# Decoder kernel, first stage: projection and finished chunk's norm moved to the chunk borders

## What is computed

```python
h_norm = _rmsnorm(h, norm1_w)
out = gate * _causal_conv(h_norm, k_base_kernel)
qk = h_norm @ jnp.concatenate((u, v), axis=1)
q, k = _l2norm(q_raw), _l2norm(k_raw)
A = jnp.einsum('bir,bjr,rij->bij', q * alpha, k, w)        # w: decays, causal mask
out = (out + jnp.einsum('bij,bjd->bid', A, h_norm)) @ proj_w.T + proj_b
h2 = residual + out
hn2 = _rmsnorm(h2, norm2_w)
mlp_out = jax.nn.gelu(hn2 @ mlp_w1 + mlp_b1) @ mlp_w2 + mlp_b2
...
x = _layernorm(x + h2 + mlp_out)                            # then cross-attention, experts
```

## Time and profile before

| | us |
|---|---|
| three runs, median (lowest to highest) | 1377.22 (1376.03 to 1378.42) |
| the profiled execution, its own time | 1376.68 |
| its span, first to last instruction | 1374.5 |
| head, to the first score matmul | 298.9 |
| PE busy in the span | 1194.8 (87%) |
| DVE, ACT, POOL busy | 886.2, 725.4, 239.2 |
| mean granted clock of PE | 0.92 |

### The profile page before, as it was taken

One profiled execution on the slowest core, in us unless ns is written; L12 is line 12 of the kernel. 1 busy time (PEld: TensorE's weight loads), 2 busy tenths in 40 slices (PEclk: granted clock), 3 DMA queues, 4 the chain that ended last, 5 costly groups with the idle time before them and its releaser, 6 DMA issues. The chain is left out here.

```text
span 1374.5 us, 19434 instructions
## 1 busy us (share of the span) xinstructions
PE 1194.8 (87%) x6246; PEld 997.2 (73%) x6246; DVE 886.2 (64%) x1988; ACT 725.4 (53%) x1279; POOL 239.2 (17%) x293
## 2 busy tenths in 40 slices
PE   4687969759999999999999999999646999999960
PEld 2465656747877778787788788788536999999960
DVE  4535343578776567877566877755665777777747
ACT  3424343637667333767433566733324777777744
POOL 1110101000000000000000000000014656666623
PEclk9788888979999999999999999999757999999985
DMA  7201000000000000000000000060560111111144
GB/s 262 70 0 46 1 24 0 24 24 1 1 0 1 32 16 8 1 0 1 32 8 11 6 0 1 1 245 31 183 215 24 47 46 42 42 42 42 46 135 133
DMA packets 45481, 63.46 MB, mean 46 GB/s; under 512 B 7201, under 2 KB 35555, under 8 KB 45283
## 3 DMA queue, kind: packets, MB, share of 16 engines
q1 hardware_dynamic: 40244, 50.52, 11.2%
q0 software_dynamic: 4416, 12.06, 2.9%
q10 hardware_dynamic: 754, 0.03, 0.0%
HBM read 50.21 MB, written 12.39 MB: 46 GB/s over the span
## 5 line engine op out<-in xcount | busy, mean ns | idle before, releaser
L77 PE MATMUL x_psum<-x_s_lo,x_kq_hi 128*128 128x512 f32 (+1 forms) x312 | 126.0, 404 | 8.0 <-PEq L241 4.3
L77 PE MATMUL x_psum<-x_p_lo,x_v_hi 128*128 128x512 f32 (+1 forms) x312 | 124.4, 399 | 0.0
L78 PE MATMUL x_psum<-x_s_hi,x_kq_lo 128*128 128x512 f32 (+1 forms) x312 | 123.4, 396 | 0.0
L79 PE MATMUL x_psum<-x_p_hi,x_v_hi 128*128 128x512 f32 (+1 forms) x312 | 123.3, 395 | 0.0
L78 PE MATMUL x_psum<-x_p_hi,x_v_lo 128*128 128x512 f32 (+1 forms) x312 | 123.3, 395 | 0.0
L79 PE MATMUL x_psum<-x_s_hi,x_kq_hi 128*128 128x512 f32 (+1 forms) x312 | 123.2, 395 | 0.0
L1186 DVE CUSTOM_DVE_ANT_0 x_e<-x_psum,x_rsb,x_rs 128x512 f32<-128x512 f32 (+1 forms) x117 | 86.4, 747 | 48.9 <-PE x_psum L79 47.9
L1036 POOL TENSOR_TENSOR x_sq<-x_sq 128x512 f32<-128x512 f32 x12 | 15.5, 1291 | 578.4 <-ACT x_sq L1022 578.4
L77 PE MATMUL e_bank<-e_w_lo,e_g_hi 128*128 128x256 f32 x368 | 107.7, 293 | 0.1
L77 PE MATMUL e_bank<-e_xT_lo,e_w_hi 128*128 128x256 f32 x368 | 105.0, 285 | 2.3 <-DVE e_xT_lo L1915 1.4
L78 PE MATMUL e_bank<-e_xT_hi,e_w_lo 128*128 128x256 f32 x368 | 104.7, 284 | 0.0
(11 more groups left out here) (353 smaller groups left out, 3284.1 us busy)
## 6 DMA issues: line engine op xcount, KB each, us to landing
w<-in_w SPq DMA_DIRECT2D x16, 1024.0 KB, 12.5
w<-scratch_results SPq DMA_DIRECT2D x8, 512.0 KB, 7.8
x_rsb<-scratch_thin_inv SPq DMA_DIRECT2D x12, 256.0 KB, 3.9
x_rsb<-scratch_thin_rs SPq DMA_DIRECT2D x9, 256.0 KB, 3.9
h_x<-in_x SPq DMA_DIRECT2D x4, 512.0 KB, 6.0
sT<-in_xT SPq DMA_DIRECT2D x4, 512.0 KB, 7.2
h_w<-in_mlp_w SPq DMA_DIRECT2D x2, 1024.0 KB, 10.3
scratch_x<-h_x SPq DMA_DIRECT2D x4, 512.0 KB, 3.3
```

What stands on the lines that cost most here:

```text
L77: pe.matmul(out, w_hi, x_lo, start=start, stop=False)
L78: pe.matmul(out, w_lo, x_hi, start=False, stop=False)
L79: return pe.matmul(out, w_hi, x_hi, start=False, stop=stop)
```

## The change

On every engine the order of the head is rewritten; the arithmetic is the same.

- `project(c + 1)` and `take_projected(c + 1)` go from f = 1 of body c to the border before it, for chunks 2 and 3: on PE behind `turn_n2`, on ACT behind `turned_hi`.
- The norm of the finished chunk goes from f = 0 to 2 of the next body to the border: `moments` behind `sums`, `factors` behind the key pieces, `apply` ahead of `turned_hi`. `roots2` leaves f = 7 for the border, and `roots1` comes ahead of `sums`.
- `norms` and `make_cats` go to f = 0, `states` joins `mask` behind the `gelu_lo` of f = 4.
- `turn_x1` writes banks 0 and 1 instead of 2 and 3, but for the last chunk. The slots' norm of chunk c - 1 uses bank 6 instead of 1.
- Key pieces 2 and 3 run before chunk 0, in banks 6 and 7; piece 0 runs ahead of `turn_cats(0)`. The borders have (4, 6), (6, 8), (8, 10), (10, 14).
- In the start-up `squares1(1)` and `roots1(1)` come earlier, `w2_hi` and `w2_lo` later, and `project(1)` runs ahead of `turn_n2(0)`.
- The context's squares start in body 1, the values' high halves in f = 5 of the last body. At the end ACT and DVE take the slots in another order.

```diff
     BEFORE = 2
-    BORDER = [(2, 6), (6, 10), (10, 12), (12, 14)]
-    PIECE_BANKS = [4, 5] + [i % 2 for i in range(len(pieces) - 2)]
+    EARLY = 4
+    BORDER = [(4, 6), (6, 8), (8, 10), (10, 14)]
+    PIECE_BANKS = [4, 5, 6, 7] + [i % 2 for i in range(len(pieces) - EARLY)]
...
+    def x1_bank(c, h):
+        return bank[2 + h] if c == LAST else bank[h]
...
             take_cats(0)
+            squares1(1)
+            squares2(0)
             act.wait_ge(ld_w2, 32)
             act.activation(w2_hi[:], w2_32[:], ACT.Copy).then_inc(w_hi_ok, 1)
-            squares2(0)
             scale_h2(0)
-            squares1(1)
+            take_projected(1)
             turned_hi(0)
-            take_projected(1)
+            for i in range(BEFORE, EARLY):
+                piece_hi(i)
...
-                    if f == 1 and c >= 1 and a < NC:
-                        take_projected(a)
...
-                    if f == 2 and c >= 1:
-                        apply(c - 1)
...
                 if a < NC:
                     scale_h2(a)
-                for i in range(*BORDER[c]):
-                    piece_hi(i)
-                if a < NC:
+                    for i in range(*BORDER[c]):
+                        piece_hi(i)
+                    apply(c)
                     turned_hi(a)
-                if c == LAST:
-                    values_hi(act, 2)
+                    if a + 1 < NC:
+                        take_projected(a + 1)
+                else:
+                    piece_hi(BORDER[c][0])
+                    piece_hi(BORDER[c][0] + 1)
+                    apply(LAST)
+                    piece_hi(BORDER[c][0] + 2)
+                    piece_hi(BORDER[c][0] + 3)
+                    values_hi(act, 3)
                     act.wait_ge(up_mm, NC * FT)
-                    for cc in range(LAST):
+                    for h in range(DH):
+                        first["slots_hi"](act, 0, 0, h)
+                    take_x1(LAST)
+                    first["slots_hi"](act, 0, LAST, 0)
+                    for cc in range(1, LAST):
...
                 for f in range(FT):
+                    if f == 0 and a < NC:
+                        norms(a)
                     gelu_lo(c * FT + f)
-                    if f == 0 and c >= 1:
-                        moments(c - 1)
-                    if f == 1 and c >= 1:
-                        factors(c - 1)
-                    if f == 2 and a < NC:
-                        norms(a)
-                    if f == 3 and a < NC:
+                    if f == 0 and a < NC:
                         make_cats(a)
-                    if f == 5 and a < NC:
+                    if f == 4 and a < NC:
                         mask(a)
+                        states(a)
                     if f == 6 and a < NC:
-                        states(a)
                         residual(a)
-                    if f == 7 and a < NC:
-                        roots2(a)
...
-                sums(c)
-                for i in range(*BORDER[c]):
-                    piece_lo(i)
                 if a < NC:
-                    turned_lo(a)
+                    roots2(a)
                     if a + 1 < NC:
                         roots1(a + 1)
                         roots1_end(a + 1)
-                if c >= 1:
-                    first["rms"](v, k, 0, c - 1, 1)
-                if c == LAST:
-                    moments(c)
+                sums(c)
+                moments(c)
+                if a < NC:
+                    for i in range(*BORDER[c]):
+                        piece_lo(i)
                     factors(c)
...
+                    turned_lo(a)
+                    if c >= 1:
+                        first["rms"](v, k, 0, c - 1)
+                else:
+                    factors(c)
...
             def turn_x1(c):
                 pe.wait_ge(x1_ok, (c + 1) * TPC)
-                pe.wait_ge(hT_lo_ok, DH * min(c + 2, NC))
-                if c >= 1:
-                    pe.wait_ge(x1_sb, DH * c)
+                if c == LAST:
+                    pe.wait_ge(hT_lo_ok, DH * NC)
+                else:
+                    pe.wait_ge(pc_ok, BORDER[c][1])
+                    pe.wait_ge(pj_sb, min(c + 3, NC) * TPC)
...
+            for i in range(BEFORE, EARLY):
+                piece(i)
+            project(1)
             turn_n2(0)
-            project(1)
...
-                    if f == 1 and c >= 1 and a < NC:
-                        project(a)
...
                 if a < NC:
                     turn_n2(a)
+                    if a + 1 < NC:
+                        project(a + 1)
```

## The result

The changed kernel takes 1330.18 us (median of four runs, 1329.15 to 1331.07), the kernel before 1376.62 us (median of four, 1374.14 to 1378.42). The ratio is 0.9664, with a 95% interval of 0.9646 to 0.9681. The forecast was 1338 in a range of 1327 to 1357. The profiled execution of the changed kernel has a span of 1328.4 us; its own time is 1330.18 us.

The account below looks back on a forecast made before the run. PE sets the head's time, waiting for operands and running at half clock after waits. Gains 4.1 + 6.3 + 15.2 + 18.5 + 6.4 + 2.2 less border losses 11.8 and 2.0 make 38.9: 1376.7 - 38.9 = 1337.8, said as 1338, range 1327 to 1357.

Parts of the forecast that it names:

- the rival on `outputs`: Bodies: the low clock behind `outputs` goes along with its wait, 3.4 us more in each of three bodies, 1328; chance 0.11.
- the baseline: Chunk bodies: a body without stalls is body 0's 42.0 less 3.96, 1.7 and 0.67 us, so 35.7 us.
- The 1.7 for a slow start after each longer border: Bodies 1 and 2: each starts at the low clock behind a longer border and loses 1.7 us.
- The rival by which the clock takes all of it back: Borders: two long idles in each bring back all the low clock lost behind waits, 1350 us; chance 0.22.
- the walk: Borders: steps of DVE's queue, then ACT's, added up from B, giving 17.4 us for borders 0 and 1, 12.1 for border 2.
- B: Borders: the end of a chunk's last down matmul; `roots2` was forecast to start 0.8 us before it.
- The last term, half a projection behind `turned_hi`: Borders 0 and 1: the last two of four projected tiles take half of 5.73 us, from B + 14.5 to B + 17.4.
- the term for `w2_lo`: Start-up: with `w2_lo` behind `roots2`, POOL's first add and `rs2` end 1.9 us earlier, between nothing and 2.28.
- 1.2 was taken for piece 0: Start-up: key piece 0 ahead of `turn_cats(0)` pulls what follows on DVE forward by 0 to 1.3 us, 1.2 taken.
- a gain of 1.0 and a bound of -1: Start-up: `project(1)` ahead of `turn_n2(0)` and `roots1(1)` moved from between `hT_hi` and `hT_lo`: gain 1.0, between 2 and -1.
- 1 to 5 at the bounds: Start-up: the first `up` comes 4.1 us earlier, near 55.1 instead of 59.2, with 1 to 5 as limits of the gain.
- The walk from the last down matmul (D): End: steps to the scores, `apply` from D + 6.0, `slots_lo` done at D + 18.5; gain 2.2 us, between 0 and 5.

Follow-up runs that it names:

- the two experiments on the states: Changed kernel with `mask` back at f = 5 and `states` at f = 6: 1335.18 us; kernel before with `states` moved from f = 6 to f = 5: 1369.53 us.

## Why the prediction was right, and where its terms were off

**Direction and mechanism: right.** The stalls went from the bodies, and the borders paid a part. The size was less so: 1330.2 us lies in the range, but in the band of the rival on `outputs` (1325 to 1332, chance 0.11) and not in the forecast's own (1332 to 1344, 0.58). Undone one by one, the projection's place is worth 22.8 us, the norm's 10.0, the early states 5.0, and `w2_lo` no more than a measurement can tell. Together that is 38 of the 46 us; the parts are not independent, so this is no full account. The norm's 10.0 hold against one place in the body only; with the transposes a step later they are gone. The place of `roots2`, the key pieces' table and the banks were not undone by themselves.

**Bodies 1 and 2: the step that failed is the baseline.** The forecast took body 0's 42.0 us and left the fall of the clock behind `outputs` in it, 3.4 us a body, as the likelier case. The rival that lets it go came nearer: without stalls a body is 42.0 - 3.96 - 1.7 - 0.67 - 3.4 = 32.3 us. The trace after agrees: body 2's 35.78, less 1.04 for `turn_x1`, 1.80 for the wait for `gelu_lo` and 1.1 for the 2.1 us that it starts at the low clock, is 31.8. The rival's reason, that the wait inside `outputs` brings the fall, is not shown: in body 1 a stretch of 3.4 us behind `outputs` still runs at the low clock without it, and the two experiments on the states lie between their theories. The 1.7 for a slow start after each longer border was too much as well (0 in body 1, 1.1 in body 2). Against it stand losses that the forecast did not have, 1.8 us of `gelu_lo` in bodies 0 and 2 among them; they hid that body 0 was off by the same 3.4. Body 3 has 27.2 us for 26.2, with 1.8 us of waits for `gelu_lo` that the sum did not have.

The rival by which the clock takes all of it back did not come. The Trainium skill's rule on a loop that makes PE wait once in every round ("TensorE: Matmul & The Clock Gate", section "HAM oscillation — how this bites in real kernels") agrees with this trace only in part: there are stretches at 0.50 in all three borders (from 98.8 us in border 0, from 146.6 and 156.8 in border 1, from 197.8 in border 2), but body 1 starts at full clock, and bodies 2 and 3 start with only 2.1 and 2.9 us at the low one.

**Borders: the walk was right, the start of the walk was not.** In border 1 `roots2` starts 0.9 us before B, each step up to `turned_hi` comes within 0.3 us of the walk, and the border has 17.37 us where the walk gave 17.4. In border 0 `roots2` starts 2.7 us before B, because B itself is late. The wait for the last `gelu_lo` is 0.8 us of that: where it is 1.8 us and the clock full, as in body 2, `roots2` starts 1.7 before B, and without it 0.9. The other 1.0 is the low clock under the last down matmuls, from 88.6 us. So each later step up to `turned_hi` is 1.5 to 1.8 us nearer to B than forecast, and the border has 15.0; that it is shorter than the walk is luck of the start and not a gain. The last term, half a projection behind `turned_hi`, was put at 2.9 and came at 2.3 and 2.9. But 0.9 of it is `turned_lo`, which the walk left out and which stands there without a projection too, so that the projection itself adds 1.4 and 2.0 us, not 2.9 each.

**Start-up: one term right, two that the clock decides.** From the end of the residual to `scale_h2` it is 6.8 us instead of 8.7; the 1.9 less are the term for `w2_lo`, and this stretch is the same in all nine kernels with that code. The residual itself ends 2.8 us earlier than before, and 1.2 to 3.7 earlier in the nine; 1.2 was taken for piece 0. From `scale_h2` to the first `up` it is 9.7 us in the changed kernel instead of 8.2, a loss of 1.6 where the forecast had a gain of 1.0 and a bound of -1. `scale_h2` before, then three rows of the kernel after:

```profile
51.05 1.71 ACT L382 ACTIVATE h_n<-h_h,h_thin 128x256 f32<-128x256 f32 x4 [7.77 <-DVEq L577]
```

```profile
46.41 1.71 ACT L388 ACTIVATE h_n<-h_h,h_thin 128x256 f32<-128x256 f32 x4 [4.09 <-DVEq L588]
...
48.56 4.21 PE L776 MATMUL x_psum<-h_pw,sT 128*128 128x288 f32 x8 [4.14 <-ACT h_hp L366]
...
56.13 0.47 PE L77 MATMUL x_psum<-h_hT_lo,h_w_hi 128*128 128x512 f32 x1 [1.65 <-DVE h_hT_lo L593]
```

Half of project(1) stands at the low clock, 4.21 us, between `scale_h2` and the transposes. But that is this trace's clock and not the order: in the kernel with `roots1` late, with the same start-up code, the pieces are slow instead, the half projection takes 2.21 us, and `up` follows `scale_h2` by 7.1, a gain of 1.0 as forecast:

```profile
40.03 6.55 PE L881 MATMUL x_psum<-h_cxT,h_wkq 128*128 128x512 f32 x8
...
47.66 1.71 ACT L388 ACTIVATE h_n<-h_h,h_thin 128x256 f32<-128x256 f32 x4 [4.09 <-DVEq L588]
...
54.76 0.47 PE L77 MATMUL x_psum<-h_hT_lo,h_w_hi 128*128 128x512 f32 x1 [1.88 <-DVE h_hT_lo L593]
```

The forecast's 55.1 lies among the 54.5 to 56.1 of the nine. Its "1 to 5 at the bounds" does not follow from the bounds of its terms, which add up to -1 and 5.6.

**End:** 18.2 for 18.9. The walk from the last down matmul (D) holds: `apply` starts at D + 6.0, and `take_x1` at D + 10.4 where the estimate had D + 10.6; the eight steps behind it are 4.3 us at 0.54 each, which makes D + 14.9 and not the 15.2 of the sum. That `slots_lo` of the last chunk waits for all seven high halves was right, as the reordered end shows (17.05 us).

## What to carry to other kernels

Before moving work out of a loop's body, ask what stands on the same engine behind it at the new place: a step put into a serial chain between two phases costs its own length, while the same step costs nothing where one short piece at a time fits between two operands that the matrix engine needs. An operand that the matrix engine must wait for cost, in this kernel, the wait and often microseconds at half clock behind it, so moving its producer earlier was worth more than the wait in the table. When a term is taken from a stretch that holds a fall of the clock, settle first whether that fall goes along with the stall: it was the largest error of the forecast.

## What the hardware showed

- DVE and POOL hold each other up, in both directions. The last `gelu_lo` of body 0 takes 2.48 us instead of 0.69, and PE waits 1.80 us for it, while POOL adds a bias into x:

```profile
85.38 2.37 POOL L336 TENSOR_TENSOR h_x<-h_x,h_b 128x1024 f32<-128x1024 f32 x1
85.82 2.48 DVE L600 TENSOR_TENSOR h_g_lo<-h_g,h_g_hi 128x512 fp32r<-128x512 f32 x1 [3.00 <-ACT h_g_hi L409]
...
88.36 0.42 PE L77 MATMUL x_psum<-h_w_lo,h_g_hi 128*128 128x256 f32 x1 [1.80 <-DVE h_g_lo L600]
```

  The DVE instruction ends 0.55 us after POOL's, about its own length, so it seems to have run after the add and not beside it at half speed. The Trainium skill ("SBUF — State Buffer", section "Who interferes with whom") says that only the port pair that DVE and GpSimd share makes them contend, and that it is an exclusive lock; the trace agrees, here and in the 4.30 us of `w2_lo`.
- The same start-up code gave a first `up` from 54.5 to 56.1 us in nine kernels. What differs is which matmuls fall into the low clock: key pieces 2 and 3 (6.55 us instead of 3.70) or half of the projection (4.21 instead of 2.21). Border 0, with the same code, took 15.0 us behind the start-up of the changed kernel and 18.5 behind one that was 1.3 us shorter, at a mean clock of 0.85 and 0.75. So the place of a low stretch moved with what ran ahead of it, and a small edit can gain 1.3 us in one stage and lose 3.5 in the next without being the reason for either. A stage's length from one trace is safe only to some 2 to 3 us here.
